# Summing the weighed experts two blocks at a time, with later loads and a new order of the queues

## The reference, cut to what matters

```python
h = tok_ref(x, token_W, pe)                 # embedding plus position of the scan
h = h + attn_ref(layernorm(h), ...)         # softmax(q k^T + rel_bias) * scale, v, projection, layernorm
h = h + ffn_ref(layernorm(h), ...)          # 8 experts, the best 2 weighed by a softmax
# ffn: gate_logits = x @ Wg + bg + bias; topk_w = softmax(top 2)
#      y = relu(x @ W1[e] + b1[e]) @ W2[e] + b2[e];  out = sum over e of combine[t, e] * y[t, e]
```

## Time and profile before

| | us |
|---|---|
| median of 3 runs | 95.45 (94.38, 95.45, 95.63) |
| profiled execution, its own time | 94.64 |
| its span, first to last instruction | 92.8 |
| busy in the span: PE, DVE, ACT, POOL | 74.9, 76.9, 69.4, 57.0 |

### The profile page before, as it was taken

The page is one execution under the profiler, slowest core; times in us unless marked ns, Lnnn a source line. Parts: engine busy times, 40 slices in busy tenths (PEclk is TensorE's granted clock), DMA queues, the critical chain, the costliest instruction groups (busy, mean ns, idle before and its releaser), DMA issues.

```text
span 92.8 us, 2790 instructions
## 1 busy us (share of the span) xinstructions
PE 74.9 (81%) x996; PEld 48.2 (52%) x1004; DVE 76.9 (83%) x305; ACT 69.4 (75%) x141; POOL 57.0 (61%) x111
## 2 busy tenths in 40 slices
...
DMA packets 5919, 3.40 MB, mean 37 GB/s; under 512 B 4914, under 2 KB 5266, under 8 KB 5906
## 3 DMA queue, kind: packets, MB, share of 16 engines
...
q10 hardware_dynamic: 512, 0.31, 1.8%
...
HBM read 2.17 MB, written 1.06 MB: 35 GB/s over the span
## 4 chain that ended last, share of the span: by engine, by line
DVE 27%; PE 20%; POOL 20%; ACT 13%; issue 10%; DMA 5%; ACTq 1%; POOLq 0%; DVEq 0%
DMA qkv_sb<-in_qkv_dram 5%; DVE pT L925 5%; POOL rs L523 4%; PE bank L1344 4%; PE bank L1371 4%; POOL half L559 3%; PE bank L1402 3%; PE bank L1353 2%; POOL rs L527 2%; ACT oneh_junk L631 2%; ACT ids_all L603 2%; POOL half L560 2%; ACT hid_lo L691 2%; ACT hid_hi L684 2%; DVE stat L769 2%
## 5 line engine op out<-in xcount | busy, mean ns | idle before, releaser
L684 ACT ACTIVATE hid_hi<-bank,b_down 128x512 f16<-128x512 f32 (+1 forms) x40 | 26.2, 658 | 3.5 <-PE bank L1344 3.1
L691 ACT ACTIVATE hid_lo<-bank,b_col 128x512 f16<-128x512 f32 (+1 forms) x40 | 26.3, 659 | 0.4 <-PE bank L1353 0.4
L1353 PE MATMUL bank<-hid_hi,minus_h 128*128 128x512 f16 (+1 forms) x40 | 14.5, 362 | 2.5 <-DVE prod L1006 1.6
L1344 PE MATMUL bank<-xT,w_hi 128*128 128x512 f16 (+1 forms) x40 | 14.3, 360 | 1.1 <-DVE h_all L952 1.0
L1344 PE MATMUL bank<-xT,w_lo 128*128 128x512 f16 (+1 forms) x40 | 14.2, 358 | 0.0
L1006 DVE TENSOR_TENSOR prod<-bank,comb 128x512 f32<-128x512 f32 x14 | 9.5, 687 | 2.5 <-POOL acc L561 1.5
L559 POOL TENSOR_TENSOR half<-prod 128x256 f32<-128x256 f32 x12 | 8.8, 737 | 2.1 <-DVE prod L1006 1.3
L1353 PEld LDWEIGHTS bank<-hid_hi,minus_h 128*128 128x128 f16 x40 | 3.9, 97 | 11.5 <-ACT hid_hi L684 9.2
L1173 PE MATMUL bank<-toe_hi,oneh_j 128*128 128x512 f16 (+3 forms) x24 | 8.3, 354 | 1.8 <-DVE pT L925 1.8
L1371 PE MATMUL bank<-w_hi,hid_hi 128*128 128x64 f16 x112 | 8.4, 193 | 0.9 <-ACT hid_lo L691 0.6
L1371 PE MATMUL bank<-w_lo,hid_hi 128*128 128x64 f16 x112 | 8.4, 193 | 0.0
...
## 6 DMA issues: line engine op xcount, KB each, us to landing
...
hankel<-in_bias_table_dram SPq DMA_DIRECT2D x1, 512.0 KB, 4.4
ids_all<-ids_scratch SPq DMA_DIRECT2D x1, 512.0 KB, 4.5
...
```

What stands on the lines that cost most here:

```text
L684: act.activation(hid_hi[:, k % 2, e, 0:m], bank[n % LBANKS][:, 0:m], ACT.Relu, bias=b1_down[:, e:e + 1], scale=KEEP * HSCALE / (XSCALE * X ...
L691: act.activation(hid_lo[:, k % 2, e, 0:m], bank[n % LBANKS][:, 0:m], ACT.Relu, bias=b1_col[:, e:e + 1], scale=HSCALE / (XSCALE * XSCALE)). ...
L1344: ins = mm(bank[n % LBANKS][:, 0:m], w[:, HID * e:HID * (e + 1)], xT[:, k % 2, 0:m], start=part == 0, stop=part == 1)
L1353: mm(bank[n % LBANKS][:, 0:m], minus_h[:], hid_hi[:, k % 2, e, 0:m], start=False, stop=True, skip_group_check=True).then_inc(s_rest, 1)
```

## The change

POOL's `gather` takes two blocks in each call, `prod` has four buffers in place of two and `half` two; `weigh(n)` waits from n = 4 on, for the pair that holds block n - 4. SP issues the load of `hankel` behind the store of the prepared ids. All five queues have a new order. Of the new lists for ACT, DVE and PE the added lines are shown; those that they replace stand in the kernel above.

```diff
@@ -226,13 +226,13 @@
...
-        prod = sb("prod", [P, 2, EXPERTS, D])
+        prod = sb("prod", [P, 4, EXPERTS, D])
...
-        half = sb("half", [P, EXPERTS // 2, D])
+        half = sb("half", [P, 2, EXPERTS // 2, D])
...
@@ -388,9 +388,9 @@
...
-            sp.dma_start(hankel[:], bass.AP(bias_table.tensor, 0, [[1, P], [1, 1024]])).then_inc(loads["hankel"], 16)
...
+            sp.dma_start(hankel[:], bass.AP(bias_table.tensor, 0, [[1, P], [1, 1024]])).then_inc(loads["hankel"], 16)
...
@@ -551,25 +551,27 @@
...
-            def gather(n):
+            def gather(k):
+
+                n = 2 * k
...
-                pool.wait_ge(s_prod, n + 1)
-                if n:
-                    pool.wait_ge(s_gather, n)
-                link(pool.tensor_tensor(half[:], prod[:, n % 2, 0:4], prod[:, n % 2, 4:8], ALU.add))
-                link(pool.tensor_tensor(half[:, 0:2], half[:, 0:2], half[:, 2:4], ALU.add))
-                last = pool.tensor_tensor(acc[:, i, :], half[:, 0], half[:, 1], ALU.add)
-                last.then_inc(s_gather, 1)
-                if i == SIZE[u] - 1 and u < LAST - 1:
+                two = slice(n % 4, n % 4 + 2)
+                pool.wait_ge(s_prod, n + 2)
+                if k:
+                    pool.wait_ge(s_gather, k)
+                link(pool.tensor_tensor(half[:], prod[:, two, 0:4], prod[:, two, 4:8], ALU.add))
+                link(pool.tensor_tensor(half[:, :, 0:2], half[:, :, 0:2], half[:, :, 2:4], ALU.add))
+                pool.tensor_tensor(acc[:, i:i + 2, :], half[:, :, 0], half[:, :, 1], ALU.add).then_inc(s_gather, 1)
+                if i + 2 == SIZE[u] and u < LAST - 1:
...
-                    pool.wait_ge(s_gather, n + 1)
+                    pool.wait_ge(s_gather, k + 1)
...
-            rsqrt_hidden(); table_values(); embed_parts(); bias_parts(); rsqrt1(0); skip_values(); value_parts()
-            rsqrt2(0); rsqrt1(1); skip_mix(); rsqrt2(1); part_low(1); part_low(2); rsqrt1(2); w2_parts(); rsqrt2(2)
-            rsqrt1(3); part_low(3); rsqrt2(3); gather(0); gather(1); rsqrt1(4); gather(2); gather(3); rsqrt2(4)
-            gather(4); gather(5); gather(6); gather(7); gather(8); gather(9); fin_parts(0); fin_parts(1); fin_parts(2)
-            fin_parts(3); fin_parts(4); gather(10); gather(11); late_pair(0); late_pair(1)
+            rsqrt_hidden(); table_values(); embed_parts(); skip_values(); rsqrt1(0); value_parts(); rsqrt2(0)
+            rsqrt1(1); bias_parts(); rsqrt2(1); skip_mix(); part_low(1); part_low(2); rsqrt1(2); w2_parts(); rsqrt2(2)
+            rsqrt1(3); part_low(3); rsqrt2(3); gather(0); rsqrt1(4); rsqrt2(4); gather(1); gather(2); gather(3)
+            gather(4); fin_parts(0); fin_parts(1); fin_parts(2); fin_parts(3); fin_parts(4); gather(5); late_pair(0)
+            late_pair(1)
...
@@ -716,19 +718,19 @@
...
+late_ids(0); late_ids(1); late_ids(2); centre_projection(); late_ids(3); centre_bias(); read_folded()
+read_hidden_rows(); count_late(0); table_exps(0); read_qk(); count_late(1); pair_exps(); read_turned_exps()
+table_exps(1); squares(0); score_tile(0); part_high(0); w1_high(); squares(1); round_rows(0); score_tile(1)
+score_tile(2); read_turned(0); score_tile(3); hidden(0, 0); hidden(0, 1); hidden(0, 2); hidden(0, 3)
+hidden(0, 4); round_rows(1); hidden(0, 5); hidden(0, 6); read_turned(1); part_high(1); choice_exp(0)
+hidden(0, 7); hidden(1, 0); part_high(2); squares(2); hidden(1, 1); choice_exp(1); hidden(1, 2)
+hidden(1, 3); hidden(1, 4); squares(3); hidden(1, 5); round_rows(2); hidden(1, 6); part_high(3)
+read_turned(2); hidden(1, 7); hidden(2, 0); hidden(2, 1); hidden(2, 2); round_rows(3); choice_exp(2)
+squares(4); hidden(2, 3); hidden(2, 4); hidden(2, 5); read_turned(3); hidden(2, 6); hidden(2, 7)
+hidden(3, 0); hidden(3, 1); round_rows(4); hidden(3, 2); hidden(3, 3); hidden(3, 4); choice_exp(3)
+read_turned(4); hidden(3, 5); hidden(3, 6); hidden(3, 7); hidden(4, 0); choice_exp(4); hidden(4, 1)
+hidden(4, 2); hidden(4, 3); hidden(4, 4); hidden(4, 5); hidden(4, 6); hidden(4, 7); read_look(0); low(4, 7)
+read_look(1); read_look(2)
@@ -1001,9 +1003,9 @@
...
-                if n >= 2:
-                    dve.wait_ge(s_gather, n - 1)
-                dve.tensor_tensor(prod[:, n % 2], bank[Y_BANK[n % 2]][:, :].rearrange("p (e d) -> p e d", d=D),
+                if n >= 4:
+                    dve.wait_ge(s_gather, n // 2 - 1)
+                dve.tensor_tensor(prod[:, n % 4], bank[Y_BANK[n % 2]][:, :].rearrange("p (e d) -> p e d", d=D),
...
@@ -1045,11 +1047,12 @@
...
-                link(dve.tensor_tensor(half_two[:], prod[:, :, 0:4], prod[:, :, 4:8], ALU.add))
+                two = slice((FIRST_BLOCK[LAST] - 2) % 4, (FIRST_BLOCK[LAST] - 2) % 4 + 2)
+                link(dve.tensor_tensor(half_two[:], prod[:, two, 0:4], prod[:, two, 4:8], ALU.add))
...
-                dve.wait_ge(s_gather, FIRST_BLOCK[LAST] - 2)
+                dve.wait_ge(s_gather, FIRST_BLOCK[LAST] // 2 - 1)
...
@@ -1066,18 +1069,18 @@
...
+constants(); id_rows(); hidden_rows(); hidden_stats(); id_columns(); table_top(); one_hot_rows(0, NQ)
+spread_values(); table_max(); late_one_hots(); table_bias(); one_hot_rows(JBLK, 2 * JBLK)
+one_hot_rows(NQ, JBLK); skip_blocks(); minus_ident(); values(); skip_columns(); penalties(); row_maxima()
+flat_weights(); skip_masks(); split_exps(); toeplitz_low(0); rows_a(0); gate_bias(); rows_b(0); key_part(0)
+rows_b2(0); part_low(0); toeplitz_low(1); rows_c(0); skip_exps(); rows_a(1); rows_d(0); w1_low(); rows_b(1)
+rows_b2(1); key_part(1); rows_c(1); choose_a(0); rows_d(1); skip_key(); key_part(2); skip_key_rows()
+choose_b(0); rows_a(2); choose_a(1); rows_b(2); rows_b2(2); key_part(3); rows_a(3); rows_c(2); choose_b(1)
+rows_d(2); rows_b(3); rows_b2(3); weigh(0); weigh(1); rows_c(3); choose_a(2); weigh(2); rows_d(3)
+rows_a(4); choose_b(2); rows_b(4); weigh(3); rows_b2(4); early_one_hots(); weigh(4); rows_c(4); weigh(5)
+rows_d(4); choose_a(3); weigh(6); choose_b(3); weigh(7); weigh(8); weigh(9); choose_a(4); choose_b(4)
+weigh(10); weigh(11); weigh_pair(0); weigh(12); weigh(13); gather_two(); weigh_pair(1); weigh_pair(2)
+sum_last_pair(); weigh_one(0); add_sixth(); weigh_one(1); add_late(); last_rows()
@@ -1429,26 +1432,26 @@
...
+turn_ids(); spread_ids(0); spread_ids(1); spread_ids(2); spread_ids(3); turn_top(); fold_weights()
...
+turn_exps(); embed(0); attend(0, 2); scores(0); weights(0); weights(1); scores(1); attend(2, 4)
+weights(2, 0, 1); scores(2); embed(1); weights(2, 1, 3); turn(0); scores(3); weights(2, 3, 4)
+first_layer(0, 0); first_layer(0, 1); first_layer(0, 2); weights(2, 4, 5); gate(0); first_layer(0, 3)
+skip_weights(); first_layer(0, 4); weights(2, 5, 8); first_layer(0, 5); skip_scores(); first_layer(0, 6)
+turn(1); weights(3, 0, 1); first_layer(0, 7); weights(3, 1, 3); first_layer(1, 0); skip_turn(); gate(1)
+attend(6, 4); first_layer(1, 1); embed(2); first_layer(1, 2); weights(3, 3, 5); first_layer(1, 3)
+weights(3, 5, 8); first_layer(1, 4); attend(10, 4); first_layer(1, 5); embed(3); first_layer(1, 6)
+second_layer(0); first_layer(1, 7); turn(2); second_layer(1); first_layer(2, 0); attend(14, 4)
+first_layer(2, 1); gate(2); first_layer(2, 2); second_layer(2); first_layer(2, 3); second_layer(3)
+first_layer(2, 4); embed(4); first_layer(2, 5); turn(3); first_layer(2, 6); second_layer(4)
+first_layer(2, 7); second_layer(5); first_layer(3, 0); first_layer(3, 1); last_bias(0); gate(3)
+first_layer(3, 2); second_layer(6); first_layer(3, 3); turn(4); first_layer(3, 4); second_layer(7)
+first_layer(3, 5); second_layer(8); first_layer(3, 6); gate(4); first_layer(3, 7); second_layer(9)
+first_layer(4, 0); first_layer(4, 1); last_bias(1); second_layer(10); first_layer(4, 2); second_layer(11)
+first_layer(4, 3); last_layer(0); last_layer(1); first_layer(4, 4); second_layer(12); first_layer(4, 5)
+second_layer(13); last_layer(2); first_layer(4, 6); look_up(0); first_layer(4, 7); last_bias(2)
+last_layer(3); last_layer(4); last_layer(5); last_bias(3); last_layer(6); take_high(EXPERTS * UNITS - 1)
+look_up(1); last_bias(4); last_layer(7); look_up(2)
```

More of the change, by code:

```diff
@@ L716, in choice_exp @@
                 act.activation(ge[:, 0:SIZE[g]], gd[:, 0:SIZE[g]], ACT.Exp).then_inc(s_ge, 1)
-            centre_projection(); late_ids(0); late_ids(1); read_folded(); late_ids(2); late_ids(3); centre_bias()
-            read_hidden_rows(); table_exps(0); read_qk(); count_late(0); count_late(1); w1_high(); table_exps(1)
-            pair_exps(); read_turned_exps(); squares(0); score_tile(0); score_tile(1); part_high(0); score_tile(2)
-            round_rows(0); squares(1); read_turned(0); score_tile(3); hidden(0, 0); hidden(0, 1); hidden(0, 2)
@@ L723, in _ @@
-            hidden(0, 3); hidden(0, 4); hidden(0, 5); round_rows(1); part_high(1); choice_exp(0); hidden(0, 6)
-            part_high(2); read_turned(1); hidden(0, 7); squares(2); hidden(1, 0); hidden(1, 1); hidden(1, 2)
```

(18 more changed lines are left out.)

21 lines of the change are left out of this document (removed).

## The result

The changed kernel takes **91.03 us** (median of 4 runs, 90.95 to 91.54) against 95.00 of the kernel before on the same chip (4 runs, 94.38 to 95.63): ratio 0.9592, 95% interval 0.952 to 0.9665. It is faster by 4.1%. Executions of the kernel before fall into a faster state (94.0 to 95.3 us in the later sets) and a slower one (95.4 to 96.3), the ratios in this document leave out those marked as slower, and since two of the four here, 95.45 and 95.63, look like slower ones but are counted in, the gain within the faster state is nearer 3.4 us than 4.0. I had said 92.8 with a range of 90.8 to 94.9, so the time lies in the range, close to its lower end. The profiled execution took 91.54 (span 89.7), against 94.64 (span 92.8) before: 3.1 us of the difference can be followed in the two traces.

A forecast was written before the change was run, and what follows sets the result against it. No engine bounds it throughout: a relay before 50 us, three nearly full engines to 65.7, PE from 67.3. A 1.6 us lead plus 0.5 gave 2.1: 92.5 from the profiled run, 93.35 from the median, so 92.8, range 90.8 to 94.9.

The forecast's parts named there:

- Everything is passed on: Rival, chance 0.12: DVE doesn't bind, PE keeps the 2.0 lead and loses the 1.61 us hole: 3.6 us, 91.0 to 91.5.
- Start: Kernel start to rsqrt1(0): hvT at 9.05, total 0.65 us sooner near 13.5, rsqrt1(0) 1.0 us sooner at 20.25.
- Hankel at 0: Later load of hankel, first read by table_exps(0): cost taken as 0, with ends 0 and 1.3 us.
- weights(0): PE's weights(0), moved between scores(0) and key_part(0): cost 0 to 0.45 us, 0.15 taken.
- Up to unit 2: Stretch to read_turned(2): 1.15 us carried of a 1.35 lead, 0.9 more at rows_d(2), lead 2.0, at about 47.6.
- 50 to 67 us: Full stretch: DVE decides, weigh(4) at 63.1 to 64.2, high(3, 2) after it; ACT and PE lead by 1.0 to 2.1, middle 1.6.
- The sums in pairs: POOL's adds of 1.26, 0.74, 0.48 us: some 3.7 us of POOL saved, off the path except two places; DVE wait worth 0 to 0.3.
- 67 us to the end: Last stretch: PE's work the same, 0.5 added to the lead, 2.1 us in all; second_layer(10) at 73.9.
- Longer holds, slower: Rival, chance 0.07: POOL's longer adds hold DVE; 97 to 98 us if all fell on DVE, decides from 4.0 us of holds.

The follow-up runs named there:

- the experiment's rows: Changed kernel with the load of hankel back at the third place of SP's queue: 91.49 us, ratio to the kernel before 0.9703.
- fin_k's wait: Changed kernel with PE's wait for the load of fin_k moved from look_up(0) to look_up(1): 90.51 us, ratio to the kernel before 0.9623.

## Why the prediction was right, and what in it was not

The total lies within the range, but not within my forecast's own 91.8 to 93.9: 91.03 is the time of the rival "Everything is passed on", to which I had given 0.12, and up to 70 us its mechanism too.

- **Start.** `rsqrt1(0)` stands at 20.17 for 20.25, and as forecast it waits for the sum of squares and not for POOL (0.83 us of idle before it). Of the terms `total` was mis-sized: it came at 12.82 for 13.5, since hvT started at 8.66 for 9.05. The kernel with `bias_parts` back shows the step by itself, and that the relay hands 1.0 us of it on.
- **Hankel at 0.** The lower end of my bounds: it landed 4.3 us after its issue (4.4 before) and ACT never waited for it. The upper end of 1.3, for which the Trainium skill (DMA: Bandwidth & Descriptors, Issuing engines are not separate DMA queues) was cited, did not come to hankel's reader. By that section hankel would share the DMA engines with w1 and w2 in place of qkv, and the trace agrees: 1.7 us longer for w1, 1.7 less for qkv, by the experiment's rows.
- **weights(0).** `key_part(0)` waited 0.29 us for it, inside 0 to 0.45. My choice of 0.15, near the fast rows, was wrong: the 2560 columns took 2.14 us (20.03 to 22.17), the slow rows' 2.1.
- **Up to unit 2.** Lead of 1.8 for 2.0, partly by luck. `rsqrt1(1)` ended with a lead of 2.06 for 1.35, because it began 0.03 us ahead of `w1_low` (27.00 and 27.03) and took 1.01 us for 1.93; at `rows_d(2)` 1.12 of it was left (46.60 against 47.72) for my 1.15, and where the other 0.9 went I haven't followed. `rows_d(2)` took 0.42 as forecast. The 0.65 us that I then took off again for `part_low(3)` at `rows_b(3)` didn't come: `og` took 0.43 there, and the step led by 2.06 (46.94 against 49.00).
- **50 to 67 us: the step that failed.** I wrote "Here DVE decides" and let `high(3, 2)` hang on `weigh(4)`. Two things are wrong in it. The size: `weigh(4)` came at 60.36, 2.7 us before the 63.1 of my sum. Of these, 0.7 are the lead of `rows_b(3)`, 2.06 for 1.35; 1.0 is `early_one_hots`, put at 2.17, the figure of a place beside POOL's sums, and done in 1.13 from start to start while POOL did `rsqrt2(4)`; and 0.9 are two holds beside POOL's sums that the sum left in: `comb` of `choose_b(2)` took 0.19 for 0.60 and `og` of `rows_b(4)` 0.42 for 0.95. The mechanism: `rows_c(4)` is ready at 61.86 and ACT comes to it at 62.35 without having waited, and with `weigh(4)` another 1.08 us sooner `round_rows(4)` doesn't move, since ACT has 17.20 us of work in 17.30. ACT and PE decide, not DVE. The slack is 0.49 us, so size and mechanism hang together: at the 2.17 of my sum `weigh(4)` would have come 1.04 later and used up more than it (an estimate from these rows). So the whole hole of 1.61 was gained on top of the lead, as in that rival.
- **The sums in pairs.** Durations right; "off the path except at two places" wrong. The new order needs the four buffers (DVE waits 7.1 us with two), and the pairing pays in the tail, by 0.35 of wait and 0.43 of hold at `fin_all` of unit 3. I had put both together at 0 to 0.3, and single sums with two buffers run 2.9 us slower.
- **67 us to the end.** I let PE pass on its lead whole. It gave back 1.1 us, mainly at the 0.96 in front of `look_up(0)`: fin_k lands some 4 us behind `fin_parts`, and PE arrives there earlier than before. The kernel before has no such idle time in front of `look_up(0)`: the load was hidden there.
- **Longer holds, slower.** They exist: gd of the units 2, 3 and 4 took 0.60, 0.61 and 1.22 us for 0.17 to 0.19 unheld. Only the last reached ACT, as 0.79 us of idle with PE still at work. They stay far below the 4.0 us from which this rival would have won.

That the total came within the range is in part luck: the lead in the full stretch was larger than my 2.1 by 1.9 us, and 1.1 that I hadn't foreseen were given back in the tail. From trace to trace I had forecast 2.1 us, the rival had 3.6, and 3.1 were measured.

What stays open: how much of the 2.2 us of `choice_exp(3)` put back lies beyond the 1.4 seen between the traces, whether hankel's place is worth anything up to 0.5, and how much of the 0.5 to 1.0 us of fin_k's wait is the changed kernel's usual cost. The new orders of DVE and PE were never put back by themselves: their share beside the steps tested is argued from the traces, not shown.
